# The tail of a two-image transformer tower: image 0's attention product ahead of image 1's on all engines

## The chip, the core and the metric

One NeuronCore of a Trainium2 chip. TensorE (PE) multiplies matrices into PSUM, eight banks of 512 fp32 columns; VectorE (DVE) and ScalarE (ACT) read PSUM and work element by element; GpSimd (POOL) does a few element-wise operations in SBUF; SyncE (SP) issues the transfers. The metric is the device time of one execution in microseconds, lower is better.

## What is computed

The first part is a two-layer vision transformer over two images (256 tokens each, width 128). The second part, the tail of the program, works on its output `h` of width 192: linear attention and a feed-forward network, each behind a normalisation and with a residual add.

```python
h = _L0_tok_ref(x, ...)                       # ends in: _ln(x, lnf_g, lnf_b) @ head_w + head_b
h = h + _L0_attn_ref(_layernorm(h), W_qkv, W_out, b_out)
h = h + _L0_ffn_ref(_layernorm(h), w_fc, w_proj, ...)

def _phi(x): return jax.nn.elu(x) + 1.0       # = max(min(exp(x), 1), x + 1)
# _L0_attn_ref, 12 heads of 16
q = _phi(q); k = _phi(k)
kv = jnp.einsum('bshd,bshm->bhdm', k, v)
z = 1.0 / (jnp.einsum('blhd,bhd->blh', q, k.sum(axis=1)) + EPS)
out = jnp.einsum('blhd,bhdm,blh->blhm', q, kv, z)
out = out @ W_out + b_out
# _L0_ffn_ref
h = new_gelu(jnp.einsum('bte,he->bth', x, W0) + b0)
out = jnp.einsum('bth,eh->bte', h, W1) + b1
```

## The kernel before

Everything is in one core; an image is two tiles (`t`) of 128 tokens. Each engine has its own list of instructions, written out by hand in order; an engine runs its list strictly in that order, and a line `engine.wait_ge(semaphore, n)` holds everything behind it on that engine. So the order of the lines is the schedule, and it is what the change edits. The two images (`i` = 0, 1) go through the same steps, interleaved.

The steps of the tail for one image, with the helper's name and the line that the profile gives:

- `turn` (L334), `gain` (ACT L1561), `head` (L446), `head_rows` (DVE L1041): the last normalisation of the first part and its head product; `h` is their result.
- `moments3`, `mean_and_variance`, `centre` (L939, L942, L959), `turn3` (L339, L340): moments, centring, transposition into a bank of 128 rows and a "rest" bank of 64 rows.
- `evict` of the rest (ACT L1558), `high_part3` (DVE L1046), `rest_low_part3` and `low_part3` (DVE L969): the transposed tile in two parts (high and low), so that the product keeps its precision. Semaphores `high3`, `low3`, later `high4`, `low4`.
- `qk3_high`, `qk3_low`, `v3_rows` (L454 to L459): query, key and value products of a tile. Banks `QK3_BANK`, `V3_BANK`.
- the features phi: `phi3_exp` (ACT L1593), `phi3_plus_one` (ACT L1597) and `phi3_max` (DVE L1056), each 128x384 for queries and keys of one tile. Their tiles lie in the memory named `embed_sb`.
- `turn_heads` of the queries (L483), `v3_to_sbuf` (ACT L1601), `context3` (L474), then `context3_masked` and `context3_sums` (DVE L1063, L1068).
- `numerators3` (L490), `denominator3`, `inverse3`, `attention3` (DVE L1077, L1081, L1084).
- `turn_heads` of the result (L483), its eviction (ACT L1558, tile `qkvw`), the output product `attend3` for each tile (L496, semaphore `out3_done`), `add_attention3` (DVE L1091).
- moments again, `inverse_deviation` on POOL (L1824), `normalise` (DVE L955), `turn3` (L339), high, rest and low parts once more.
- feed-forward: `fc3(i, c)`, six slices of five matmuls (L503 to L507), `gelu3` (ACT L1607) and `proj3(i, c, t)` (L510), then `add_ff3` (DVE L1095) and the stores.

In the order before, TensorE runs image 1's query, key and value products among image 0's attention, both tiles of image 0's output product before VectorE adds either, then image 1's features and context, and only then image 0's feed-forward slices, between which image 1's attention ends. VectorE makes image 1's high and low parts before image 0's denominator, and adds the attention of image 0 only when both tiles are done (`out3_done` 2).

## Time and profile before

| | us |
|---|---|
| median of three runs | 129.16 (128.75 to 129.81) |
| the profiled execution's own time | 129.22 |
| its span in the profile | 126.8 |
| PE busy | 117.3 (93%) |
| DVE busy | 77.0 (61%) |
| ACT busy | 62.9 (50%) |
| POOL busy | 45.9 (36%) |

The span reaches from the first instruction of the program to the last; the time of an execution has some 2.4 us around it. The granted clock of TensorE is 1.00 throughout, its higher level of 2.4 GHz. A row of the timeline gives the start in us from the span's beginning, the length, the engine, the line, what is written from what, the shape and how many instructions were merged; in square brackets stands the idle time of the engine ahead of it and who ended it. Matmuls overlap: the start of the next one, not the end of this one, tells how long TensorE was taken.

### The profile page before, as it was taken

What the parts mean: (1) busy time and instruction counts of PE and PEld (TensorE: products, weight loads), DVE (VectorE), ACT (ScalarE), POOL (GpSimd) and SP (SyncE); (2) the same over time, 40 slices, a digit from 0 to 9 for tenths busy, and PEclk for the clock granted to TensorE, in tenths of its full rate; (3) what the DMA queues carried; (4) which work ended last, traced back from release to release, by engine and by line L of the source; (5) the groups of instructions that cost most, each with busy time, mean ns of one, the idle gap of its engine ahead of it and who ended that gap; (6) DMA issues with size and microseconds to landing.
All of it is one profiled execution on the core that took longest, in us unless ns stands there. A gap on an engine that the chain in (4) does not pass through costs nothing.

```text
span 126.8 us, 2258 instructions
## 1 busy us (share of the span) xinstructions
PE 117.3 (93%) x852; PEld 101.2 (80%) x852; DVE 77.0 (61%) x244; ACT 62.9 (50%) x151; POOL 45.9 (36%) x56
## 2 busy tenths in 40 slices
PE   6999979999999999999999899977989988999991
PEld 6989968985978778997856689966777877998990
DVE  5000264996787766679999897639498377155002
ACT  4000142844579478194774876534871735423520
POOL 0000024034599833204939858475214032031000
PEclk9999999999999999999999999999999999999999
DMA  4999799999600000000000000000000000000101
GB/s 106 353 418 433 228 435 393 386 421 414 185 0 0 0 3 5 0 0 0 0 0 5 0 0 0 3 5 0 0 0 0 0 0 5 0 0 0 62 0 62
DMA packets 4171, 12.43 MB, mean 98 GB/s; under 512 B 473, under 2 KB 2105, under 8 KB 3906
## 3 DMA queue, kind: packets, MB, share of 16 engines
q1 hardware_dynamic: 4162, 12.31, 26.0%
q8 instruction: 6, 0.10, 0.3%
q14 instruction: 3, 0.02, 0.1%
HBM read 11.91 MB, written 0.39 MB: 97 GB/s over the span
## 4 chain that ended last, share of the span: by engine, by line
PE 65%; DVE 12%; DMA 9%; ACT 4%; issue 3%; SPq 3%; POOL 2%; DVEq 0%; ACTq 0%; POOLq 0%
DMA norm_rows_sb<-in_norm_rows 9%; PE bank L405 6%; PE bank L510 6%; PE bank L424 5%; PE bank L381 4%; PE bank L325 4%; PE bank L398 3%; PE bank L376 3%; SPq L265 3%; PE bank L346 3%; PE bank L412 2%; PE bank L358 2%; PE bank L496 2%; PE bank L334 2%; PE bank L390 2%
## 5 line engine op out<-in xcount | busy, mean ns | idle before, releaser
L1824 POOL TENSOR_TENSOR rstd<-mv,minus_half 128x2 f32<-128x2 f32 x14 | 10.0, 716 | 47.8 <-DVE mv L942 47.8
L1842 POOL TENSOR_TENSOR qn<-q,rqsum 128x512 f32<-128x512 f32 x8 | 8.3, 1042 | 10.5 <-DVE rqsum L1012 10.5
L1607 ACT ACTIVATE patches_sb<-bank,fcb 128x256 f32<-128x256 f32 x12 | 5.1, 469 | 10.5 <-PE bank L507 10.5
L1565 ACT ACTIVATE kexp<-bank,nkmax 128x256 f32<-128x256 f32 x16 | 7.5, 472 | 5.7 <-DVE nkmax L992 5.7
L405 PEld LDWEIGHTS bank<-cw,qT 128*128 128x128 f32 x64 | 8.0, 191 | 2.4 <-issue 1.5
L405 PE MATMUL bank<-cw,qT 128*128 128x128 f32 x64 | 8.9, 280 | 0.7 <-DVE x L1027 0.4
L510 PE MATMUL bank<-projw,patches_sb 128*128 128x192 f32 x48 | 9.4, 331 | 0.0
L325 PE MATMUL bank<-embed_sb 128*128 128x128 f32 x64 | 8.7, 291 | 0.3 <-DMA embed_sb<-in_embed 0.3
L424 PE MATMUL bank<-restw,hid 128*128 128x128 f32 x64 | 8.8, 281 | 0.1
L325 PEld LDWEIGHTS bank<-embed_sb 128*128 128x128 f32 x64 | 8.0, 200 | 1.1 <-DMA embed_sb<-in_embed 1.1
L1558 ACT ACTIVATE x<-bank 128x128 f32<-128x128 f32 x4 | 1.1, 282 | 14.4 <-DVE stats L936 14.4
L1581 ACT ACTIVATE hid<-bank,small_sb 128x256 f32<-128x256 f32 x16 | 6.5, 472 | 3.6 <-PE bank L419 3.6
L424 PEld LDWEIGHTS bank<-restw,hid 128*128 128x128 f32 x64 | 7.8, 191 | 0.6 <-issue 0.3
L936 DVE BATCH_NORM_STATS2 stats<-bank 128x6 f32<-128x128 f32 x4 | 1.1, 274 | 11.7 <-PE bank L330 11.6
L510 PEld LDWEIGHTS bank<-projw,patches_sb 128*128 128x128 f32 x48 | 7.6, 189 | 0.5 <-ACT patches_sb L1607 0.4
L381 PE MATMUL bank<-ktok,y 128*128 128x512 f32 x16 | 8.0, 612 | 0.0
L325 PE MATMUL bank<-embed_sb,patches_sb 128*128 128x128 f32 x64 | 7.9, 277 | 0.0
L325 PEld LDWEIGHTS bank<-embed_sb,patches_sb 128*128 128x128 f32 x64 | 7.5, 192 | 0.2 <-DMA patches_sb<-in_patches 0.2
L992 DVE TENSOR_REDUCE nkmax<-bank 128x2 f32<-128x512 f32 x8 | 5.4, 688 | 3.0 <-PE bank L365 2.9
L1834 POOL TENSOR_TENSOR xb<-x,rows_sb 128x256 f32<-128x256 f32 x8 | 5.8, 730 | 3.6 <-DVE xn L978 2.4
L969 DVE TENSOR_TENSOR yT_lo<-bank,yT_hi 128x256 fp32r<-128x256 f32 x12 | 5.1, 422 | 2.9 <-ACT yT_hi L1558 2.8
L1577 ACT ACTIVATE cw<-bank,rksum 128x128 f32<-128x128 f32 x16 | 4.8, 364 | 3.8 <-PE bank L398 3.8
(165 smaller groups left out, 333.0 us busy)
## 6 DMA issues: line engine op xcount, KB each, us to landing
embed_sb<-in_embed SPq DMA_DIRECT2D x3, 768.0 KB, 7.7
patches_sb<-in_patches SPq DMA_DIRECT2D x2, 1024.0 KB, 12.5
restw<-in_rest_w SPq DMA_DIRECT2D x2, 768.0 KB, 15.6
qkvw<-in_qkv_w SPq DMA_DIRECT2D x3, 256.0 KB, 11.7
qkvw<-in_qkv_w SPq DMA_DIRECT2D x1, 768.0 KB, 15.7
fcw<-in_fc_w SPq DMA_DIRECT2D x1, 768.0 KB, 18.3
embed_sb<-in_embed SPq DMA_DIRECT2D x1, 576.0 KB, 4.4
aqkvw<-in_aqkv_w SPq DMA_DIRECT2D x1, 576.0 KB, 12.2
```

The source lines that it names most:

```text
L325: mm = nc.tensor.matmul(CONV_BANK[i][t][:, 0:D], left, embed_sb[:, c, 0:D], start=(c == 0), stop=False)
L381: return nc.tensor.matmul(YK_BANK[s][:], y[s % IMAGES][:, t, :], ktok[:, t, :], start=(t == 0), stop=(t == TILES - 1))
L405: mm = nc.tensor.matmul(ATT_BANK[s][t][:, 0:D], qT[:, t, c * P:(c + 1) * P], cw[:, c, :], start=(c == 0), stop=(c == PAIRS - 1))
L424: mm = nc.tensor.matmul(FF2_BANK[s][t][:, 0:D], hid[:, c, t * P:(t + 1) * P], ff2w(s // IMAGES, c), start=(c == 0), stop=(c == FC - 1))
L510: return nc.tensor.matmul(PROJ3_BANK[i][t][:, 0:E], hid3[i][:, c, t * P:(t + 1) * P], projw[:, c, :], start=(c == 0), stop=(c == HC - 1))
L969: return nc.vector.tensor_tensor(lo, exact, hi.bitcast(F32), ALU.subtract)
L992: return nc.vector.tensor_reduce(nkmax[i][:, 2 * b:2 * b + 2], K_BANK[s][b][:].rearrange("p (c t) -> p c t", c=2), AX_X, ALU.max, negate=True)
L1565: return nc.scalar.activation(kexp[:, c, :], K_BANK[s][c // 2][:, (c % 2) * TOKENS:(c % 2 + 1) * TOKENS], ACT.Exp, bias=nkmax[i][:, c:c + ...
L1581: return nc.scalar.activation(hid[:, c, :], FF1_BANK[s][c // 2][:, (c % 2) * TOKENS:(c % 2 + 1) * TOKENS], ACT.Gelu, bias=col("ff1_b", s / ...
L1824: return nc.gpsimd.tensor_tensor(rstd[i][:], mv[i][:, :, 1], minus_half[:], ALU.pow)
L1834: return nc.gpsimd.tensor_tensor(xb[i][:], x[i][:], row.unsqueeze(1).to_broadcast([P, TILES, D]), ALU.add)
L1842: return nc.gpsimd.tensor_tensor(qn[:, t, :].rearrange("p (h d) -> p h d", h=HEADS), q[:, t, :].rearrange("p (h d) -> p h d", h=HEADS), rq ...
```

## The change

Only the tail is edited, from image 0's query and key products on.

- VectorE does two operations that ScalarE did: `phi3_plus_one(0, 0)` and `gain(1)`, with semaphores of their own (`phi3_plus_one_first`, `head_in_second`). ScalarE does one that VectorE did: the high part of image 0's second transposition (`evict(yT3_hi[0])`), so that `high4` comes from ScalarE for image 0 and `high4_second` from VectorE for image 1.
- TensorE runs image 0's value products before image 1's last transposition and head, image 0's numerators before `turn3(1)`, image 0's transposition of the attention and its output product before image 1's query and key products are complete, `turn3` of image 0's second normalisation before image 1's query transposition, and `fc3(0, 0)`, `fc3(0, 1)` before image 1's context. Image 1's context, numerators, transposition and output product stand between slices and projections of image 0.
- VectorE does image 0's context masks before image 1's moments, its denominator and attention before image 1's high and low parts, its add and second normalisation before image 1's features.
- `add_attention3(i, t)` waits for one tile (`out3_done` 1, 2, 3, 4) and so runs a tile at a time; the two tiles' products lie in different banks (`ATT3_BANK`).
- Banks of `TURN4`, `Q3` and `ATT3` move so that the new order has free banks.

```diff
@@ banks
-        TURN4_BANK = [bank[3], bank[5]]
+        TURN4_BANK = [bank[2], bank[5]]
-        Q3_BANK = [bank[6], bank[3]]
+        Q3_BANK = [bank[6], bank[1]]
-        ATT3_BANK = [bank[2], bank[7]]
+        ATT3_BANK = [(bank[2], bank[4]), (bank[7], bank[4])]
@@ TensorE
             qk3_low(0, 0).then_inc(qk3_done, 1)
+            qk3_low(0, 1).then_inc(qk3_done, 1)
+            v3_rows(0, 0).then_inc(v3_done, 1)
             pe.wait_ge(centred_last, 4)
             turn(TURNF_BANK[1], xn[1]).then_inc(last_turned, 1)
-            qk3_low(0, 1).then_inc(qk3_done, 1)
-            pe.wait_ge(head_in_ready, 2)
+            v3_rows(0, 1).then_inc(v3_done, 1)
+            pe.wait_ge(head_in_second, 1)
             head(1, 0).then_inc(head_done, 1)
...
+            pe.wait_ge(attention3_ready, 2)
+            turn_heads(AT3_BANK[0], att3[0]).then_inc(attention3_turned, 1)
             pe.wait_ge(high3, 2)
             qk3_high(1, 0)
-            pe.wait_ge(low3, 2)
-            qk3_low(1, 0).then_inc(qk3_done, 1)
             qk3_high(1, 1)
-            pe.wait_ge(attention3_ready, 2)
-            turn_heads(AT3_BANK[0], att3[0]).then_inc(attention3_turned, 1)
-            qk3_low(1, 1).then_inc(qk3_done, 1)
             pe.wait_ge(attention3_columns, 1)
             pe.wait_ge(loaded["aout"], 16)
             attend3(0, 0).then_inc(out3_done, 1)
             attend3(0, 1).then_inc(out3_done, 1)
...
             pe.wait_ge(low4, 1)
             fc3(0, 0).then_inc(fc3_done, 1)
             fc3(0, 1).then_inc(fc3_done, 1)
+            pe.wait_ge(v3_ready, 4)
+            context3(1).then_inc(context3_done, 1)
+            fc3(0, 2).then_inc(fc3_done, 1)
+            pe.wait_ge(q3_columns, 2)
+            pe.wait_ge(context3_ready, 4)
+            numerators3(1).then_inc(numerators3_done, 1)
+            fc3(0, 3).then_inc(fc3_done, 1)
+            pe.wait_ge(gelu3_ready, 1)
+            proj3(0, 0, 0).then_inc(proj3_done, 1)
+            pe.wait_ge(gelu3_ready, 2)
+            proj3(0, 0, 1).then_inc(proj3_done, 1)
             pe.wait_ge(attention3_ready, 4)
             turn_heads(AT3_BANK[1], att3[1]).then_inc(attention3_turned, 1)
-            fc3(0, 2).then_inc(fc3_done, 1)
-            pe.wait_ge(gelu3_ready, 1)
-            proj3(0, 0, 0).then_inc(proj3_done, 1)
+            proj3(0, 1, 0).then_inc(proj3_done, 1)
             pe.wait_ge(attention3_columns, 2)
             attend3(1, 0).then_inc(out3_done, 1)
             attend3(1, 1).then_inc(out3_done, 1)
...
@@ VectorE
+            def gain(i, bankof):
+                return nc.vector.tensor_scalar(yT[i], bankof[:, 0:TOKENS], col("lnf_g"), None, ALU.mult)
+            def phi3_plus_one(i, t):
+                return nc.vector.tensor_scalar(qk3p[i][:, t, :], QK3_BANK[i][t][:, 0:2 * E], rstd[i][:, t:t + 1], 1.0,
+                                               ALU.mult, ALU.add)
...
+            dve.wait_ge(phi3_exp_ready, 1)
+            phi3_plus_one(0, 0).then_inc(phi3_plus_one_first, 1)
+            dve.wait_ge(last_turned, 2)
+            gain(1, TURNF_BANK[1]).then_inc(head_in_second, 1)
...
-            dve.wait_ge(out3_done, 2)
+            dve.wait_ge(out3_done, 1)
             add_attention3(0, 0).then_inc(h_mid, 1)
-            add_attention3(0, 1).then_inc(h_mid, 1)
             dve.wait_ge(h_mid, 1)
             moments3(0, 0).then_inc(moments4_done, 1)
+            dve.wait_ge(out3_done, 2)
+            add_attention3(0, 1).then_inc(h_mid, 1)
...
@@ ScalarE
+            act.wait_ge(turned4, 1)
+            evict(yT3_rest[0][0:EB, :], TURN4_REST_BANK[0][0:EB, 0:TOKENS]).then_inc(rest_high4, 1)
+            evict(yT3_hi[0][:], TURN4_BANK[0][:, 0:TOKENS]).then_inc(high4, 1)
```

Three places of the order, before and of the change. Line numbers of the changed kernel are two or more higher for the same helper.

TensorE, where image 1's context product stands (L474 before, L476 now, from `v31`): before, it follows the transposition of image 1's queries (L483) and comes ahead of image 0's second transposition (L339, L340), image 1's numerators (L490) and image 0's first feed-forward slice (L503 on).

```order
L483 MATMUL bank3<-small_sb,embed_sb 96x128 x4
L474 MATMUL bank6<-v31,embed_sb 96x102 x4
L339 MATMUL bank3<-small_sb,xn0 128x128
L340 MATMUL bank4<-small_sb,xn0 64x128
L339 MATMUL bank3<-small_sb,xn0 128x128
L340 MATMUL bank4<-small_sb,xn0 64x128
L490 MATMUL bank6<-kv31,patches1_sb 128x102 x4
L503 MATMUL bank3<-yT3_hi0,fcw_hi 128x256
L504 MATMUL bank3<-yT3_hi0,fcw_lo 128x256
```

In the change:

```order
L485 MATMUL bank1<-small_sb,embed_sb 96x128 x4
L505 MATMUL bank3<-yT3_hi0,fcw_hi 128x256
L506 MATMUL bank3<-yT3_hi0,fcw_lo 128x256
L507 MATMUL bank3<-yT3_lo0,fcw_hi 128x256
L508 MATMUL bank3<-yT3_rest0,fcw_hi 128x256
L509 MATMUL bank3<-yT3_rest0,fcw_lo 128x256
L505 MATMUL bank3<-yT3_hi0,fcw_hi 128x256
L506 MATMUL bank3<-yT3_hi0,fcw_lo 128x256
L507 MATMUL bank3<-yT3_lo0,fcw_hi 128x256
L508 MATMUL bank3<-yT3_rest0,fcw_hi 128x256
L509 MATMUL bank3<-yT3_rest0,fcw_lo 128x256
L476 MATMUL bank6<-v31,embed_sb 96x102 x4
```

Image 0's first two feed-forward slices (ten matmuls, bank 3) now stand ahead of the context product of image 1.

VectorE, where image 0's denominator stands (`den30`, L1077 before, L1086 now): before, behind the high, rest and low parts of image 1 (`yT3_hi1`, `yT3_rest1`, `yT3_lo1`).

```order
L1063 TENSOR_TENSOR kv30<-bank1,small_sb 96x2x96
L1068 SCALAR_TENSOR_TENSOR kv30<-bank1,small_sb 96x2x6
L1046 CAST yT3_hi1<-bank0 128x256
L969 TENSOR_TENSOR yT3_rest1<-bank6,yT3_rest1 64x256
L969 TENSOR_TENSOR yT3_lo1<-bank0,yT3_hi1 128x256
L1077 TENSOR_SCALAR den30<-bank1 128x24
L1081 RECIPROCAL z30<-den30 128x24
L1084 TENSOR_TENSOR embed_sb<-bank1,z30 128x192 x2
```

In the change:

```order
L1072 TENSOR_TENSOR kv30<-bank1,small_sb 96x2x96
L1077 SCALAR_TENSOR_TENSOR kv30<-bank1,small_sb 96x2x6
L944 BN_AGGR mv1<-stats31 128x2
L941 BN_STATS stats31<-h1 128x6
L944 BN_AGGR mv1<-stats31 128x2
L961 TENSOR_SCALAR xn1<-h1,mv1 128x192 x2
L1086 TENSOR_SCALAR den30<-bank1 128x24
L1090 RECIPROCAL z30<-den30 128x24
L1093 TENSOR_TENSOR embed_sb<-bank1,z30 128x192 x2
```

Image 1's moments and centring (`stats31`, `mv1`, `xn1`) are now between the context sums and the denominator, and image 1's three parts have moved behind image 0's attention (L1093).

ScalarE, where the transposed attention of image 0 is evicted (tile `qkvw0`): before, between the features of image 1 (plus-one L1597, exponential L1593).

```order
L1597 ACTIVATE embed_sb<-bank3,ones,rstd1 128x384
L1593 ACTIVATE embed_sb<-bank3,rstd1 128x384
L1558 ACTIVATE qkvw0<-bank5 96x512
L1593 ACTIVATE embed_sb<-bank7,rstd1 128x384
L1597 ACTIVATE embed_sb<-bank7,ones,rstd1 128x384
```

In the change it comes ahead of all four of them:

```order
L1572 ACTIVATE qkvw0<-bank5 96x512
L1611 ACTIVATE embed_sb<-bank3,ones,rstd1 128x384
L1607 ACTIVATE embed_sb<-bank3,rstd1 128x384
L1607 ACTIVATE embed_sb<-bank7,rstd1 128x384
L1611 ACTIVATE embed_sb<-bank7,ones,rstd1 128x384
```

The features of image 1 (L1611, L1607) wait behind the eviction now.

## Rows read from the trace of the kernel before

**Rows 1.** Windows: stretch, its us, busy PE, PEld, DVE, ACT, POOL, granted clock, DMA.

```profile
104.00:112.00 8.00, 7.41 (x55) 6.80 (x54) 4.38 (x16) 3.71 (x7) 0.99 (x1) 1.00 0.01 2
112.00:120.00 8.00, 7.97 (x58) 7.58 (x59) 2.53 (x8) 2.99 (x8) 1.71 (x2) 1.00 0.08 25
```

**Rows 2.** Timeline: features of image 0's first tile, ScalarE and VectorE; columns as told above.

```profile
90.41 0.58 ACT L1593 ACTIVATE embed_sb<-bank,rstd 128x384 f32<-128x384 f32 x1 [0.52 <-PE bank L459]
...
90.89 0.47 ACT L1561 ACTIVATE y<-bank,small_sb 128x256 f32<-128x256 f32 x1
91.25 1.24 ACT L1597 ACTIVATE embed_sb<-bank,ones,rstd 128x384 f32<-128x384 f32 x2
...
91.95 0.56 DVE L1056 SCALAR_TENSOR_TENSOR embed_sb<-embed_sb 128x384 f32<-128x384 f32 x1 [1.80 <-ACT embed_sb L1597]
```

**Rows 3.** Timeline: image 0 from query transposition to its first feed-forward slice.

```profile
93.75 0.64 PE L483 MATMUL bank<-small_sb,embed_sb 128*96 128x128 f32 x4 [0.33 <-DVE embed_sb L1056]
93.94 0.19 DVE L942 BATCH_NORM_AGGREGATE mv<-stats 128x2 f32<-128x9 f32 x1
...
94.56 0.51 DVE L959 TENSOR_SCALAR xn<-h,mv 128x192 f32<-128x192 f32 x2
...
95.71 1.14 PE L490 MATMUL bank<-kv,patches_sb 96*128 96x102 f32 x8
...
97.06 0.17 DVE L1077 TENSOR_SCALAR den<-bank 128x24 f32<-128x24 f32 x1
...
98.28 0.64 PE L483 MATMUL bank<-small_sb,embed_sb 128*96 128x128 f32 x4
...
99.07 0.58 ACT L1558 ACTIVATE qkvw<-bank 96x512 f32<-96x512 f32 x1
...
99.71 1.57 PE L496 MATMUL bank<-aoutw,qkvw 96*128 96x192 f32 x8 [0.26 <-ACT qkvw L1558]
...
101.31 0.62 DVE L1091 TENSOR_TENSOR h<-bank,hb 128x192 f32<-128x192 f32 x2
...
101.85 0.61 DVE L939 BATCH_NORM_STATS2 stats<-h 128x6 f32<-128x192 f32 x2
...
102.38 0.31 DVE L942 BATCH_NORM_AGGREGATE mv<-stats 128x2 f32<-128x9 f32 x2
...
104.23 0.33 PE L339 MATMUL bank<-small_sb,xn 128*128 128x128 f32 x1
...
105.81 0.42 DVE L969 TENSOR_TENSOR yT_lo<-bank,yT_hi 128x256 fp32r<-128x256 f32 x1
...
106.29 0.39 PE L503 MATMUL bank<-yT_hi,fcw_hi 128*128 128x256 f32 x1 [0.49 <-DVE yT_lo L969]
```

**Rows 4.** Timeline: image 1 from its context product to its feed-forward and projections.

```profile
103.20 0.94 PE L474 MATMUL bank<-v,embed_sb 128*96 128x102 f32 x8 [0.39 <-ACT v L1601]
...
104.72 1.08 PE L490 MATMUL bank<-kv,patches_sb 96*128 96x102 f32 x8
...
108.90 1.49 PE L496 MATMUL bank<-aoutw,qkvw 96*128 96x192 f32 x8
...
111.87 0.20 DVE L942 BATCH_NORM_AGGREGATE mv<-stats 128x2 f32<-128x9 f32 x1
...
114.41 0.27 PE L339 MATMUL bank<-small_sb,xn 128*128 128x128 f32 x1
...
116.42 0.39 PE L503 MATMUL bank<-yT_hi,fcw_hi 128*128 128x256 f32 x1
...
118.81 2.11 PE L510 MATMUL bank<-projw,patches_sb 128*128 128x192 f32 x12
```

**Rows 5.** Timeline of ScalarE alone, around image 0's second transposition.

```profile
104.92 0.38 ACT L1558 ACTIVATE yT_rest<-bank 64x256 fp32r<-64x256 f32 x1 [1.30 <-PE bank L340]
105.32 1.28 ACT L1607 ACT_TABLE_LOAD   x1
```

93 lines of the change are left out of this document (41 added, 52 removed).

## The prediction

> **What bounds the kernel now.** I read the busy time by windows first. From 112 to 120 us TensorE is busy 7.97 us of 8 [rows 1]: there its own work sets the time, and only the start of that stretch can move. So I then read the timeline of the tail row by row, with what ended each wait, to see what sets that start. The last piece, image 1's six slices of the feed-forward product (L503 to L507) and its projections (L510), starts at 116.42 and runs to the end of the 126.8 us span without a wait that counts [rows 4]; nothing in it changes. So the forecast is one question: when does the first L503 of image 1 start in the changed kernel? The 10.38 us behind it are kept, and so are the 2.42 us that the profiled execution's own time (129.22 us) has over its span. That execution lies 0.06 us above the median of the runs, 129.16.
>
> Two chains lead there. Image 0's: features, transpose (L483), context, numerators (L490), denominator (L1077), attention, transpose, eviction, output product (L496), add (L1091), moments, normalisation, transpose (L339), high and low parts, first L503 at 106.29 [rows 3]. Image 1's goes the same way one lap later and ends at 116.42 [rows 4]. Before the change they are interleaved so that image 1's context product runs at 103.20, before image 0's feed-forward [rows 4].
>
> **Image 0's leg, walked with the new order.** Each hand-over is counted at the 0.03 to 0.06 us that the rows show between the end of one and the start of the next.
>
> Features: the first exponential ends at 90.99; then ScalarE does the gain and two plus-ones, and VectorE's first maximum waits 1.80 us for them, until 91.95 [rows 2]. Now VectorE does the first plus-one itself, from 91.02. No row has this form there; bounds are 0.56 (its own 128x384 maximum, from SBUF) and 0.62 (ScalarE's plus-one, 1.24 for two) [rows 2]; I take 0.58, nearer to the row of the same engine. The gain follows. Its bounds are 0.42 (VectorE's low part, 128x256 from PSUM [rows 3]) and 0.47 (ScalarE's own gain [rows 2]); I take 0.42. It also waits for image 1's transpose, which now stands behind the value product's first half on TensorE; I allow 0.15 for that (an estimate: eight matmuls stand ahead of it on TensorE), so a plus-one at its upper bound would cost nothing more. Two maxima, together 1.04: the transpose L483 starts at 93.27 instead of 93.75, 0.48 earlier.
>
> Perfetto Trace Analysis of the Trainium skill (Optimizing Scalar/DVE Operations) gives VectorE about 125 ns of overhead per instruction on PSUM and ScalarE about 51, which speaks against moving these two PSUM reads to VectorE. By it the moved gain would take 0.07 more than ScalarE's 0.47, 0.54 in all, and the leg would win 0.36 instead of 0.48, an estimate from that page. The rows here do not agree: VectorE's 256 columns from PSUM take 0.42 against ScalarE's 0.47.
>
> Numerators at 95.71 - 0.48 = 95.23, ending 1.14 later at 96.37 [rows 3]. Before, the denominator stood behind image 1's high, rest and low parts and started at 97.06. Now only image 1's moments and centring stand there, which took from 93.94 to 95.07 [rows 3], 1.13 us; started behind the context sums (95.2) they end just in time. So the denominator starts at 96.41, 0.65 earlier. To the transpose 1.22 (97.06 to 98.28), the transpose 0.64: eviction at 98.31 instead of 99.07, where it had stood behind an exponential of image 1. Output product at 98.95, 0.76 earlier.
>
> The add by tile: the product of both tiles takes 1.57; the first half of its eight matmul records is done after some 0.85. So the first add and its moments lie beside the second half. Behind the second tile's end (100.56) come one add 0.35, one moments 0.35, one mean 0.19 (the pairs' 0.62, 0.61 and 0.31 [rows 3], each of two that overlap by some 0.08) and two hand-overs: 101.53. Before, it was 102.69 [rows 3]. The lead is 1.16 us. Reciprocal deviation, normalisation and transpose are the same: L339 at 103.07. From there to L503 took 2.06 us [rows 3]. ScalarE now evicts the high part behind the rest, 0.38 each [rows 5], done 0.76 after the transpose; VectorE needs it for the low part only 0.89 after (104.92 to 105.81 [rows 3, 5]), so this costs nothing; were it 0.3 slower, 0.2. Image 0's first L503: 106.29 - 1.16 = 105.13.
>
> **Image 1's leg pays.** On TensorE its context product now stands behind the wait for image 0's low part and two feed-forward slices. Four slices take 2.39 us (116.42 to 118.81), so two take 1.20 [rows 4]: context at 106.33 instead of 103.20, 3.13 later. To its numerators 1.52, these 1.08: denominator at 108.97. 1.22 to the transpose, 0.64 for it, eviction 0.58, hand-overs 0.10: output product at 111.51 instead of 108.90. Here TensorE waits twice, about 0.2 before the transpose and 0.5 before the product, since the slices and projections put between them are shorter than the chain through VectorE and ScalarE.
>
> Then the add by tile gives part back: product 1.49, add, moments and mean as above, 114.01 instead of 112.07, that is 1.94 late. With 1.54 more, as from 102.69 to 104.23 [rows 3], the transpose could go at 115.55. TensorE is free a little later: from the product to that transpose it had 5.51 us of work (108.90 to 114.41), of which one slice (0.60) and two projections (twelve records in 2.11, two to a projection: 0.35 each) are done before now; 111.51 + 4.2 = 115.7. Before, the transpose ran at 114.41, 0.8 after its input was there, so the chain had slack; now it has none. Transpose 1.14 to 1.29 late; last L503 block at 117.56 to 117.71. I take the middle, **1.2 us later**.
>
> The other edits cost nothing: the table load of 1.28 [rows 5] now stands behind image 1's query eviction, some 0.3 us later than before, and its cover is that the first projection waits behind two more slices and two products of image 1; without that cover it would cost at most these 0.3. The moved banks only let the order be. GpSimd's and SP's queues keep their order.
>
> **The rivals.**
> 1. *Forecast: image 1's chain sets the end.* 129.22 + 1.2, rounded to the tenth above since hand-overs that no row has can only be longer than the shortest ones: 130.5; by the bounds (gain, plus-one, 0.03 or 0.06 at some fourteen hand-overs, the two ends above) 130.0 to 130.9.
> 2. *TensorE's work alone sets it, no change to be told.* If image 1's two waits (0.2 + 0.5) vanish because VectorE and ScalarE have nothing else there, TensorE still has the 10.13 us of 106.29 to 116.42 [rows 3, 4], plus image 1's context and numerators, about 0.8 + 0.9 (their 0.94 and 1.08 [rows 4] without the last records' drain, which the next matmul overlaps), which came before image 0's first slice and now come behind it. That is 105.13 + 11.8 = 116.9, or 0.5 late, and some 0.2 less for waits inside the 10.13: 129.5. For it speaks that TensorE is full from 112 [rows 1]; against it, that denominator to product takes 2.5 us by the rows and only some 1.9 us of work stands there.
> 3. *Faster.* Image 0's lead is larger, because VectorE's features and the overlapped add take less than I count. It decides at image 0's first L503: that must start before 104.6 (lead 1.7 or more) for the TensorE sum of rival 2 to end before 116.42, and at 103.3 the run is 1% faster, 127.9. Against it: the longest terms of the leg (0.64, 0.58, 1.57, 2.06) are unchanged instructions.
> 4. *The lead is not had, or the chain is longer.* If image 0's lead shrinks to 0.5 (the maxima wait for TensorE's turn, or the denominator for image 1's centring), every later time moves by 0.7: 131.1. The centring has only 0.1 us to spare there.
>
> **How the numbers follow.** Rival 1 0.58, rival 2 0.18, rival 3 0.08, rival 4 0.16. A difference of about 1% (1.3 us) is what a measurement of this kernel can tell from none; that line lies at 130.45 here, in the middle of the forecast's own range. So slower is 0.58 x 0.6 + 0.15 = 0.50; same is 0.58 x 0.4 + 0.18 + 0.01 = 0.42; faster 0.08. The range takes in rival 2 below and rival 4 above: 129.4 to 131.4, leaving out about 1 in 10 on each side.
>
> **What would show it.** In the profile after: image 0's L503 (there L505) near 105.1; image 1's context product behind two slices, near 106.3; TensorE waiting for VectorE's attention and for ScalarE's eviction of image 1, 0.7 together; image 1's transpose without slack behind the normalisation; image 1's first slice near 117.6, and the same 10.4 us behind it. I am wrong if that slice starts before 116.9, if image 0's lead is not about 1.2, or if VectorE's plus-one takes over 0.8. The granted clock should stay at 1.00 as in rows 1.

## The result, and the profile after

| | before | after |
|---|---|---|
| median of the runs | 128.98 us (128.67 to 129.81) | 130.24 us (130.01 to 131.99) |
| ratio to before | | 1.010 (95% interval 1.0075 to 1.0125) |
| span of the profiled execution | 126.8 us | 128.0 us |
| image 0's first feed-forward slice | 106.29 [rows 3] | 104.97 |
| image 1's first feed-forward slice | 116.42 [rows 4] | 117.59 |

The changed kernel is 1.0% slower. Image 0 is 1.32 us earlier, image 1 is 1.17 us later, and image 1 is the last. In two of the 11 executions of the changed kernel the mean granted clock was 0.987 instead of 1.00, and these took 131.22 and 131.99 us, the upper end of its row.

In the profile after, the line numbers are a few higher: L341 is the transpose, L485 the turn of heads, L476 the context, L492 the numerators, L498 the output product, L505 the first matmul of a feed-forward slice, L512 a projection, L1572 ScalarE's evictions. The two stretches of [rows 1], windows with busy PE, PEld, DVE, ACT, POOL, then granted clock and DMA:

```profile
104.00:112.00 8.00, 7.20 (x54) 6.19 (x55) 2.38 (x8) 4.75 (x11) 0.69 (x1) 1.00 0.01 2
112.00:120.00 8.00, 7.95 (x59) 7.51 (x59) 4.04 (x13) 2.06 (x6) 1.70 (x2) 1.00 0.08 25
```

From 112 us TensorE is as full as before, and the clock stays at its upper level: what was lost was lost ahead of that. The timeline of the features and of image 0 (start, us, engine, line, operation, what ended the wait ahead of it), which answers to [rows 2, 3]:

```profile
90.42 1.09 ACT L1607 ACTIVATE embed_sb<-bank,rstd 128x384 f32<-128x384 f32 x2 [0.52 <-PE bank L461]
...
91.11 0.62 DVE L1060 TENSOR_SCALAR embed_sb<-bank,rstd 128x384 f32<-128x384 f32 x1 [0.95 <-ACT embed_sb L1607]
...
91.42 0.66 ACT L1611 ACTIVATE embed_sb<-bank,ones,rstd 128x384 f32<-128x384 f32 x1
...
91.69 0.48 DVE L1057 TENSOR_SCALAR y<-bank,small_sb 128x256 f32<-128x256 f32 x1
...
92.10 1.02 DVE L1065 SCALAR_TENSOR_TENSOR embed_sb<-embed_sb 128x384 f32<-128x384 f32 x2
...
93.17 0.64 PE L485 MATMUL bank<-small_sb,embed_sb 128*96 128x128 f32 x4
...
95.12 1.11 PE L492 MATMUL bank<-kv,patches_sb 96*128 96x102 f32 x8 [0.61 <-DVE kv L1077]
...
96.27 0.18 DVE L1086 TENSOR_SCALAR den<-bank 128x24 f32<-128x24 f32 x1 [0.30 <-PE bank L492]
...
97.50 0.64 PE L485 MATMUL bank<-small_sb,embed_sb 128*96 128x128 f32 x4 [0.82 <-DVE embed_sb L1093]
...
98.18 0.59 ACT L1572 ACTIVATE qkvw<-bank 96x512 f32<-96x512 f32 x1 [1.09 <-PE bank L485]
...
98.82 1.57 PE L498 MATMUL bank<-aoutw,qkvw 96*128 96x192 f32 x8
...
101.22 0.20 DVE L944 BATCH_NORM_AGGREGATE mv<-stats 128x2 f32<-128x9 f32 x1
...
102.95 0.33 PE L341 MATMUL bank<-small_sb,xn 128*128 128x128 f32 x1 [0.43 <-DVE xn L957]
...
104.97 0.39 PE L505 MATMUL bank<-yT_hi,fcw_hi 128*128 128x256 f32 x1 [0.43 <-DVE yT_lo L971]
```

Image 0's chain now runs link by link, and TensorE waits at each: 0.61 ahead of the numerators and 0.82 ahead of the turn of the attention, where in the kernel before image 1's work stood. Image 1, which answers to [rows 4]:

```profile
106.22 0.86 PE L476 MATMUL bank<-v,embed_sb 128*96 128x102 f32 x8
...
108.84 0.18 DVE L1086 TENSOR_SCALAR den<-bank 128x24 f32<-128x24 f32 x1 [1.29 <-PE bank L492]
...
110.07 0.64 PE L485 MATMUL bank<-small_sb,embed_sb 128*96 128x128 f32 x4
...
111.39 1.57 PE L498 MATMUL bank<-aoutw,qkvw 96*128 96x192 f32 x8 [0.35 <-ACT qkvw L1572]
...
113.79 0.20 DVE L944 BATCH_NORM_AGGREGATE mv<-stats 128x2 f32<-128x9 f32 x1
...
114.80 0.67 DVE L957 TENSOR_SCALAR xn<-h,mv,rstd 128x192 f32<-128x192 f32 x2 [0.81 <-POOL rstd L1836]
...
115.58 0.28 PE L341 MATMUL bank<-small_sb,xn 128*128 128x128 f32 x1
...
117.59 0.39 PE L505 MATMUL bank<-yT_hi,fcw_hi 128*128 128x256 f32 x1
```

The context is 3.02 us later than before, the output product 2.49, the transpose 1.17. The normalisation ends at 115.47 and the transpose follows at 115.58. In the kernel before, the normalisation ended at 113.55, and the transpose at 114.41 followed only 0.86 us later; that slack is gone.

```profile
112.88 0.67 DVE L955 TENSOR_SCALAR xn<-h,mv,rstd 128x192 f32<-128x192 f32 x2 [0.82 <-POOL rstd L1824]
```

### The profile page after: what moved, and what is told of

Its sections match the earlier page's. It is cut to its first block, busy times and chain, and to the rows that moved or that the text cites. A ratio compares the mean times of both kernels' runs of the same rounds, so it can differ in the third digit from the quotient of the medians.

```text
span 128.0 us, 2259 instructions
## 1 busy us (share of the span) xinstructions
PE 117.1 (92%) x852; PEld 101.3 (79%) x852; DVE 77.7 (61%) x245; ACT 62.2 (49%) x150; POOL 46.6 (36%) x56
## 4 chain that ended last, share of the span: by engine, by line
PE 63%; DVE 12%; DMA 12%; SPq 5%; issue 3%; ACT 2%; POOL 1%; ACTq 0%
DMA patches_sb<-in_patches 12%; PE bank L407 6%; PE bank L426 5%; SPq L267 5%; PE bank L512 5%; PE bank L383 4%; PE bank L400 3%; PE bank L327 3%; PE bank L378 3%; PE bank L414 2%; PE bank L336 2%; PE bank L498 2%; PE bank L348 2%; PE bank L492 2%; PE bank L392 2%
## 5 line engine op out<-in xcount | busy, mean ns | idle before, releaser
L512 PE MATMUL bank<-projw,patches_sb 128*128 128x192 f32 x48 | 9.2, 329 | 0.0
L1572 ACT ACTIVATE x<-bank 128x128 f32<-128x128 f32 x4 | 1.1, 282 | 14.4 <-DVE stats L938 14.4
L512 PEld LDWEIGHTS bank<-projw,patches_sb 128*128 128x128 f32 x48 | 7.7, 189 | 0.3 <-ACT patches_sb L1621 0.2
```

The lines of the kernel that those rows point to most:

```text
L512: return nc.tensor.matmul(PROJ3_BANK[i][t][:, 0:E], hid3[i][:, c, t * P:(t + 1) * P], projw[:, c, :], start=(c == 0), stop=(c == HC - 1))
```

## The experiments

Two executions can differ by some tenths of a us ahead of the part that is changed. So beside the ratio of the runs to those of the kernel before, a table gives the **tail** of each profiled execution: from image 0's first transpose (87.53 in the changed kernel) to the end of the last add of the program (125.11 + 0.68 there). It is worked out from those two rows of each trace, so it stands for one execution. From the first transpose to image 1's output product the changed kernel, less_after and tile_back_1 run the same code, and their traces give 23.86, 23.89 and 23.92 us; differences of under 0.1 us say nothing.

| kernel | median us, ratio to before (95%) | tail us | against before |
|---|---|---|---|
| before | | 37.09 | |
| after | 130.24, 1.010 (1.0075 to 1.0125) | 38.26 | +1.17 |
| less_after | 130.23, 1.0086 (1.0052 to 1.0119) | 38.33 | +1.24 |
| less_before | 128.66, 0.9947 (0.9926 to 0.9969) | 36.57 | -0.52 |
| ctx_early | 129.43, 1.000 (0.9972 to 1.0027) | 37.09 | 0.00 |
| tile_back_1 | 130.86, 1.0135 (1.0101 to 1.0169) | 38.87 | +1.78 |
| filled | 130.50, 1.0111 (1.0079 to 1.0143) | 38.35 | +1.26 |
| feat_act | 132.28, 1.0201 (1.0155 to 1.0248) | 40.90 | +3.81 |
| tile_back | 131.96, 1.0153 (1.0111 to 1.0195) | 40.87 | +3.78 |
| high_dve | 130.90, 1.0109 (1.0063 to 1.0155) | 38.42 | +1.33 |
| tile_before | 129.17, 0.9991 (0.9967 to 1.0015) | 37.25 | +0.16 |
| feat_before | 129.51, 1.0021 (0.9990 to 1.0052) | 37.38 | +0.29 |
| pulled | 127.64, 0.9868 (0.9842 to 0.9895) | 35.68 | -1.41 |
| pulled_act | 129.27, 1.0016 (0.9980 to 1.0051) | 37.27 | +0.18 |

The theory of the prediction (A) is that image 1's attention chain sets the end. Its rival (B) is that TensorE's own work does, because image 1's context and numerators now stand behind image 0's first slices.

**Take work from TensorE.** Four projection matmuls left out between image 1's output product and its transpose, in both kernels.

```diff
-            proj3(0, 1, 1).then_inc(proj3_done, 1)
...
-            proj3(0, 2, 0).then_inc(proj3_done, 1)
-            proj3(0, 2, 1).then_inc(proj3_done, 1)
...
-            proj3(0, 3, 0).then_inc(proj3_done, 1)
```

> The changed kernel without four matmuls of image 0's second projection (hidden chunks 1 to 3: tile 1 of chunk 1, both tiles of chunk 2, tile 0 of chunk 3), which TensorE does between image 1's output product and image 1's transpose turn3(TURN4[1]); what they would add to image 0's output is left out. Each takes 0.32 to 0.33 us there, so TensorE has 1.3 us less to do ahead of that transpose. Theory A (image 1's attention chain sets the end): the two normalise instructions end at 115.47 us in the changed kernel and the transpose starts at 115.58; with less work in front it still starts at 115.5 to 115.6, TensorE waits about 1.3 us there, and the span stays 127.9 to 128.0 us (ratio to the kernel before 1.01). Theory B (TensorE's own work sets the end, since context and numerators of image 1 now stand behind the first fc3): the transpose starts at about 114.3 and the span is 126.7 (ratio 1.00).

> The kernel before without the same four matmuls of image 0's second projection (what they would add to image 0's output is left out): 1.3 us less for TensorE between image 1's output product and the transpose turn3(TURN4[1]). In the kernel before the two normalise instructions end near 113.6 us and the transpose starts at 114.41, so the chain has 0.75 us to spare there and TensorE's work is what comes last. Theory A: the transpose moves to where the chain allows it, about 113.65 to 113.7, and 0.7 of the 1.3 us comes back: span about 126.1 (ratio 0.994). Theory B: all 1.3 us come back, span 125.5 (ratio 0.99).

The rows with a wait, of less_after (the normalisation and the transpose) and then of less_before (a slice of image 0):

```profile
114.46 0.67 DVE L953 TENSOR_SCALAR xn<-h,mv,rstd 128x192 f32<-128x192 f32 x2 [0.82 <-POOL rstd L1832]
...
115.18 0.33 PE L341 MATMUL bank<-small_sb,xn 128*128 128x128 f32 x1 [1.05 <-DVE xn L953]
```

```profile
112.44 0.36 PE L503 MATMUL bank<-yT_hi,fcw_hi 128*128 128x256 f32 x1 [0.70 <-ACT patches_sb L1603]
```

In the changed kernel 1.3 us less work bought nothing: TensorE stood still for 1.05 us of it, waiting for image 1's normalisation. That is theory A: less work for TensorE does not help. But it was nearly a tie. Here the transpose starts 0.05 us behind the end of the normalisation (115.13), in the changed kernel 0.11 behind it, and without a wait of TensorE. So from the output product to the transpose (4.19 us) TensorE's work and the chain end within some 0.06 us of each other; the chain's lead is ahead of that, in the 0.35 us that TensorE waits for the product. In the kernel before the same cut bought 0.52 us, less than the 0.7 expected: behind the cut TensorE waited 0.70 us for ScalarE's GELU of image 0, a wait that I had not counted. So this run does not measure the slack of image 1's chain in the kernel before; it shows only that TensorE's work counts there.

**Bring image 1's chain forward.** In the changed kernel, context ahead of the first slice, ScalarE's values ahead of its evictions, numerators one slice earlier.

```diff
+            pe.wait_ge(v3_ready, 4)
+            context3(1).then_inc(context3_done, 1)
             pe.wait_ge(low4, 1)
...
-            pe.wait_ge(v3_ready, 4)
-            context3(1).then_inc(context3_done, 1)
-            fc3(0, 2).then_inc(fc3_done, 1)
...
+            fc3(0, 2).then_inc(fc3_done, 1)
```

> The changed kernel with image 1's context matmuls ahead of image 0's first fc3 (directly behind the turn of image 1's query features), the two evictions of image 1's values on ScalarE ahead of the evictions of image 0's second transpose, and image 1's numerators behind the second fc3 instead of the third. Image 0's lead up to there is kept. ScalarE is free at 103.12, so the values are there by 103.85, the context can run at 104.4 instead of 106.22, its masks at about 105.3, the numerators at 106.4 to 106.6 instead of 107.69. Theory A: the rest of image 1's chain moves with them as far as TensorE has room: its attention is turned about 0.9 us earlier, the output product at about 110.5 instead of 111.39, the last transpose at about 114.7 instead of 115.58, and the span is 127.0 to 127.3: most of the loss is undone (ratio to the kernel before 1.002 to 1.004). Theory B: only the 0.43 us for which TensorE waits ahead of the first fc3 is filled, and 0.2 of it is lost again because fc3's operands come later: span 127.6 to 128.0 (ratio 1.007 to 1.01).

TensorE's timeline of this kernel:

```profile
104.26 0.86 PE L476 MATMUL bank<-v,embed_sb 128*96 128x102 f32 x8
104.90 0.36 PE L505 MATMUL bank<-yT_hi,fcw_hi 128*128 128x256 f32 x1
...
106.16 1.03 PE L492 MATMUL bank<-kv,patches_sb 96*128 96x102 f32 x8
...
110.14 1.57 PE L498 MATMUL bank<-aoutw,qkvw 96*128 96x192 f32 x8 [0.35 <-ACT qkvw L1572]
...
114.32 0.28 PE L341 MATMUL bank<-small_sb,xn 128*128 128x128 f32 x1
```

The context starts 1.96 us earlier than in the changed kernel, the output product 1.25, the transpose 1.26, and the whole loss is gone: the tail is that of the kernel before. Theory A, and by more than I expected: I had thought TensorE short of room, but it still waits 0.35 ahead of the product. It also shows what image 0's lead is worth: its first slice starts at 104.90 here, 1.39 earlier than before (1.29 when counted from the first transpose), and the end is where it was.

**Lengthen image 1's chain.** In the changed kernel, image 1's attention added only when both tiles are there.

```diff
-            dve.wait_ge(out3_done, 3)
+            dve.wait_ge(out3_done, 4)
             add_attention3(1, 0).then_inc(h_mid, 1)
+            add_attention3(1, 1).then_inc(h_mid, 1)
```

> The changed kernel with image 1's attention alone added when both tiles' output products are done; image 0's adds stay by tile. Image 0's lead and everything up to image 1's output product stay as in the changed kernel. From the start of that product to the last transpose TensorE is never idle in the changed kernel (111.39 to 115.58, 4.19 us), and without four projections it waited 1.05 us there, so chain and work end within 0.25 us of each other. Theory A (image 1's chain sets the end): the chain behind the product is longer by the 0.4 to 0.67 us between the two adds, the last transpose starts 4.5 to 4.85 us behind the product's start, and the span is 128.3 to 128.7. Theory B (TensorE's own work alone): 4.19 us as before, span 128.0.

TensorE, image 1's product and transpose:

```profile
110.95 1.57 PE L498 MATMUL bank<-aoutw,qkvw 96*128 96x192 f32 x8 [0.35 <-ACT qkvw L1571]
...
115.67 0.33 PE L341 MATMUL bank<-small_sb,xn 128*128 128x128 f32 x1 [0.35 <-DVE xn L957]
```

From product to transpose 4.72 us against 4.19, and the tail is 0.61 longer: a longer chain behind the product moves the end, as A has it. Since chain and work were a tie there, this shows that the chain has no slack, not that the work has any.

**Put work into the waits of image 0's chain.** Three idle matmuls.

```diff
             context3(0).then_inc(context3_done, 1)
+            warm_up(bank[5], 1)
...
+            warm_up(bank[5], 2)
             pe.wait_ge(attention3_ready, 2)
```

> The changed kernel with three more matmuls on ones into a bank that is free there, whose result nobody reads: one in the 0.61 us for which TensorE waits ahead of image 0's numerators, two in the 0.82 us ahead of the turn of image 0's attention; each takes TensorE 0.32 to 0.33 us at full clock, 0.97 together. Theory A (TensorE's waits in image 0's chain are the chain's, and work put into them is free): numerators, turn and all behind them start when they did, span 127.9 to 128.1. Rival (TensorE's total work counts): span 128.9 to 129.0. Beside it, for the granted clock: in the changed kernel without image 0's features on VectorE TensorE waited 1.27, 0.61 and 0.82 us between 93 and 98.6 and its clock was 0.50 from 100 to 102; if such waits are what the clock falls after, the fuller stretch shows 1.00 throughout.

TensorE's timeline of this kernel, the added matmuls (L318) and the two links that waited:

```profile
94.15 0.51 PE L318 MATMUL bank<-ones 128*128 128x192 f32 x2
94.93 1.11 PE L492 MATMUL bank<-kv,patches_sb 96*128 96x102 f32 x8 [0.27 <-DVE kv L1079]
96.33 0.82 PE L318 MATMUL bank<-ones 128*128 128x192 f32 x4
97.31 0.64 PE L485 MATMUL bank<-small_sb,embed_sb 128*96 128x128 f32 x4 [0.17 <-DVE embed_sb L1095]
```

The matmuls (two records each) take up most of both waits, and the tail is longer by only 0.09 us. Work is free there. This is the room that image 1's work filled in the kernel before.

**What each edit is worth in the changed order.** First the features back on ScalarE, then both images' adds together, then image 0's high part on VectorE.

```diff
             phi3_exp(0, 0).then_inc(phi3_exp_ready, 1)
+            act.wait_ge(last_turned, 2)
+            gain(1, TURNF_BANK[1]).then_inc(head_in_ready, 1)
+            phi3_plus_one(0, 0).then_inc(phi3_plus_one_ready, 1)
```

> The changed kernel with the two moved feature instructions (one of image 0's plus-one tiles, and image 1's gain) back on ScalarE in their old order, all else as changed. In the kernel before the turn of image 0's query features starts at 93.75, in the changed one at 93.17. Theory A (image 1's chain hangs on the first fc3, which hangs on image 0's chain): the whole row of links is later by the 0.58 us or a little more, since image 0's features now stand directly in front of everything else: first fc3 at 105.5 or later, span 128.6 or more (ratio 1.014 or more). Theory B (TensorE's work behind the first fc3 sets the end and image 0's lead is slack): nothing changes by more than 0.2 us, span 127.9 to 128.2.

```diff
-            dve.wait_ge(out3_done, 1)
+            dve.wait_ge(out3_done, 2)
             add_attention3(0, 0).then_inc(h_mid, 1)
+            add_attention3(0, 1).then_inc(h_mid, 1)
```

> The changed kernel with both images' attention added only when the output products of both tiles are done, as in the kernel before; all else as changed. In the changed kernel the first add of image 0 starts at 99.78, the second at 100.45, and the last mean at 101.42 ends 0.97 us behind the second add's start; in the kernel before that stretch, both adds in one, took 1.38 us ([rows 3]: 101.31 to 102.69). So each image's chain is longer by 0.4 us, or by up to 0.67 if the first add's whole head start is lost. Theory A (image 1's chain sets the end and hangs on image 0's): both count, span 128.8 to 129.3 (0.8 to 1.3 us more than the changed kernel's 128.0). Theory B (TensorE's own work sets the end): image 0's lead and image 1's chain have slack, span 127.9 to 128.3.

```diff
+            dve.wait_ge(turned4, 1)
+            high_part3(0, TURN4_BANK[0]).then_inc(high4, 1)
...
-            evict(yT3_hi[0][:], TURN4_BANK[0][:, 0:TOKENS]).then_inc(high4, 1)
```

> The changed kernel with the high part of image 0's second transposed tile on VectorE again (0.42 us there, 0.36 on ScalarE), all else as changed. VectorE waits 0.22 us for ScalarE's eviction of the rest in front of its two low parts (104.06 and 104.49), ready since 103.85. With the high part in front, VectorE would do it from 103.85 (behind its second maximum) to 104.2, and the low parts at 104.25 and 104.7: the first fc3 is 0.1 to 0.25 us later. Theory A (the prediction's: the moved eviction is worth at most what VectorE waits, and image 1's chain follows the first fc3): span 128.0 to 128.25. Rival: the edit matters by its full 0.42 us, since low parts, fc3 and all of image 1 follow: span 128.4.

In the profiled executions of feat_act and of tile_back TensorE's granted clock fell, so their tails hold more than the edits. Windows of feat_act, then of tile_back:

```profile
98.00:100.00 2.00, 1.44 (x7) 1.43 (x8) 1.68 (x5) 0.64 (x2) 0.33 (x1) 0.70 0.00 0
100.00:102.00 2.00, 2.00 (x8) 2.00 (x7) 0.00 (x0) 0.10 (x1) 0.00 (x0) 0.50 0.00 0
```

```profile
104.00:106.00 2.00, 1.31 (x8) 1.05 (x9) 1.04 (x3) 1.97 (x6) 1.06 (x1) 0.94 0.00 0
106.00:108.00 2.00, 2.00 (x13) 2.00 (x12) 0.00 (x0) 1.51 (x3) 0.00 (x0) 0.50 0.00 0
```

Ahead of the fall both can be read. In feat_act the turn of image 0's query features starts 6.88 us behind the first transpose instead of 5.64: 1.24 later, more than the 0.58 expected, because in TensorE's new order ScalarE waits for image 1's turn ahead of its gain:

```profile
91.50 0.47 ACT L1570 ACTIVATE y<-bank,small_sb 128x256 f32<-128x256 f32 x1 [0.69 <-PE bank L336]
```

In tile_back image 0's transpose starts 4.73 us behind its output product (98.59 to 103.32) instead of 4.13, 0.60 later. There is no trace of these two kernels without the fall, but each has four executions at a granted clock of 1.00, with spans of 128.8 to 130.0 us (feat_act, median 129.6) and 128.6 to 129.9 (tile_back, 129.0); the medians of the kernel before beside them are 127.1 and 127.0. That is 2.5 and 2.0 us over the kernel before, where the changed kernel has 1.2: undoing the features costs some 1.3 us and undoing the adds some 0.8, with a spread of half a us. Both agree with A (128.6 or more; 128.8 to 129.3), and B's 128.3 at most is out. The high part on VectorE costs 0.16 us by the tail, within A's 0 to 0.25, too little for the ratio to tell.

**One edit alone in the order before.**

```diff
-        ATT3_BANK = [bank[2], bank[7]]
+        ATT3_BANK = [(bank[2], bank[4]), (bank[7], bank[4])]
...
-            dve.wait_ge(out3_done, 2)
+            dve.wait_ge(out3_done, 1)
```

> The kernel before with one part of the change alone: the attention added by tile (two banks for each image's output product), all orders else as before. Theory A (a link is worth something only where its chain is last): in the kernel before VectorE is at image 1's maximum until 101.3 when image 0's products come, so nothing starts earlier there, and in image 1 the last transpose waits for TensorE's own work, with 0.75 us to spare; gain between 0 and 0.1 us, or a loss of up to 0.2 by the new waits between VectorE's own instructions: span 126.7 to 127.0. Rival (the edit shortens each image's chain by 0.4 us or more wherever it stands): span 126.0 to 126.4.

```diff
+            phi3_plus_one(0, 0).then_inc(phi3_plus_one_first, 1)
+            dve.wait_ge(last_turned, 2)
+            gain(1, TURNF_BANK[1]).then_inc(head_in_second, 1)
...
-            gain(1, TURNF_BANK[1]).then_inc(head_in_ready, 1)
-            phi3_plus_one(0, 0).then_inc(phi3_plus_one_ready, 1)
```

> The kernel before with one part of the change alone: image 0's features as in the changed kernel (one plus-one tile and image 1's gain on VectorE, both maxima ahead of image 1's head rows, TensorE's order in this stretch as changed), all from the turn of image 0's query features on as before. That turn then starts about 0.58 us earlier, as in the changed kernel (93.17 against 93.75). Theory A (a link gains only where its chain is last): image 1's head rows, means and centre come behind both maxima on VectorE, as in the changed kernel, where the transpose of image 1 that needs them started 96.07 against 95.17; in the old order that transpose stands ahead of image 0's numerators, so TensorE waits there for 0.5 to 1 us and the lead is gone by the numerators: span 126.7 to 127.2, no gain. Rival (the 0.58 us go through to the end): span 126.2.

TensorE in feat_before:

```profile
93.36 0.64 PE L485 MATMUL bank<-small_sb,embed_sb 128*96 128x128 f32 x4
93.84 0.86 PE L476 MATMUL bank<-v,embed_sb 128*96 128x102 f32 x8
95.62 0.33 PE L341 MATMUL bank<-small_sb,xn 128*128 128x128 f32 x1 [0.92 <-DVE xn L961]
```

Neither gains: the ratios take in 1, the tails are 0.16 and 0.29 longer. In feat_before the turn does start 0.59 earlier (5.64 against 6.23 us behind the first transpose), and behind the context product TensorE then waits 0.92 us for image 1's centre.

**The opposite order.** Image 1 as close behind image 0 as its operands allow, image 0's remaining slices and projections behind that. Kept from the change: image 0's plus-one tile and the gain on VectorE, the adds by tile, the high eviction of image 0 on ScalarE, the banks. New here: one plus-one tile of image 1 on VectorE too, and the projections of both images interleaved at the end. TensorE's order against the kernel before, around the two images' attention:

```diff
             context3(1).then_inc(context3_done, 1)
-            pe.wait_ge(normalised4, 2)
-            pe.wait_ge(q3_columns, 2)
-            turn3(TURN4_BANK[0], TURN4_REST_BANK[0], xn[0]).then_inc(turned4, 1)
...
             numerators3(1).then_inc(numerators3_done, 1)
+            pe.wait_ge(normalised4, 2)
+            turn3(TURN4_BANK[0], TURN4_REST_BANK[0], xn[0]).then_inc(turned4, 1)
             pe.wait_ge(attention3_ready, 4)
             turn_heads(AT3_BANK[1], att3[1]).then_inc(attention3_turned, 1)
+            pe.wait_ge(low4, 2)
+            fc3(0, 1).then_inc(fc3_done, 1)
+            fc3(0, 0).then_inc(fc3_done, 1)
...
             attend3(1, 0).then_inc(out3_done, 1)
```

> The opposite order, with the same helpers and banks as the changed kernel: image 1's features, context, masks, numerators, attention and output product are pulled up as close behind image 0's as its operands allow (context of image 1 directly behind the turn of its query features, its numerators ahead of image 0's second transpose, its attention's turn ahead of image 0's first fc3, its output product behind two fc3 instead of four units of work), image 0's remaining fc3 and projections fill TensorE behind that, and the two images' projections are interleaved at the end. Some parts are kept from the change (one plus-one tile and the gain on VectorE, the high eviction of image 0 on ScalarE, the adds by tile). Theory A (the end is set by the later of image 1's chain and TensorE's work; with image 1 early, TensorE's work alone is left): in the kernel before TensorE waits about 0.6 us for image 1's values ahead of its context, 0.6 ahead of the first fc3 and 0.8 in front of image 0's turns and numerators; some 1 to 1.7 us of these close up, and the last transpose of image 1, ready 2 to 3 us earlier, is never waited for: span 125.1 to 126.0 (ratio 0.985 to 0.993). Theory B (only the work that stands behind the first fc3 counts, and image 0's early start is what shortens the program): image 0's output product and first fc3 come no earlier than in the kernel before, so nothing is gained: span 126.6 or more.

TensorE's timeline of this kernel:

```profile
101.41 0.86 PE L476 MATMUL bank<-v,embed_sb 128*96 128x102 f32 x8
102.79 1.14 PE L492 MATMUL bank<-kv,patches_sb 96*128 96x102 f32 x8 [0.52 <-DVE kv L1073]
...
105.20 0.64 PE L485 MATMUL bank<-small_sb,embed_sb 128*96 128x128 f32 x4 [0.80 <-DVE embed_sb L1089]
105.98 0.38 PE L505 MATMUL bank<-yT_hi,fcw_hi 128*128 128x256 f32 x1
...
111.49 0.27 PE L341 MATMUL bank<-small_sb,xn 128*128 128x128 f32 x1
```

This kernel beats both, by 1.3% against the one before. Image 1's context starts at 101.41 (before 103.20, after 106.22) and its last transpose at 111.49 (before 114.41, after 115.58), while image 0's first slice, at 105.98, is a full microsecond later than in the changed kernel. Behind 105.20 no row of TensorE shows a wait up to the last add. The span, 125.2, is what A expected (125.1 to 126.0), and not B's 126.6; and image 1's transpose is not waited for, as A said.

But A's sum was another: 1 to 1.7 us of TensorE's waits were to close up. Windows over the tail, of the kernel before, the changed kernel and pulled:

```profile
87.52:124.61 37.09, 34.34 (x234) 30.13 (x234) 18.93 (x64) 17.29 (x35) 7.00 (x9) 1.00 0.02 6
87.53:125.79 38.26, 34.30 (x234) 30.21 (x234) 19.62 (x65) 16.63 (x34) 7.71 (x9) 1.00 0.02 6
87.54:123.22 35.68, 32.94 (x234) 30.29 (x234) 20.21 (x66) 16.28 (x33) 7.00 (x9) 1.00 0.02 7
```

The changed kernel's loss is all in TensorE's idle time (38.26 - 34.30 = 3.96 against 2.75 us), but pulled's idle time is 2.74, as before. Its gain is in busy time, 1.40 us less for the same 234 records of matmuls. A busy row can hide a short stall, since the ends of matmuls are modelled: in the kernel before, 0.36 us pass from the projection at 116.06 to the next matmul, instead of the usual 0.16, and the rows show no wait of that length. The 48 records of projections, which pulled also puts in another order, are 0.6 of the 1.40, counted from start to start. So that image 1's early chain alone makes the gain is not shown; the interleaved projections were not run by themselves.

Then the same kernel with the three moved feature instructions (one plus-one tile of each image, and the gain) back on ScalarE:

```diff
             phi3_exp(0, 0).then_inc(phi3_exp_ready, 1)
+            act.wait_ge(last_turned, 2)
+            gain(1, TURNF_BANK[1]).then_inc(head_in_ready, 1)
+            phi3_plus_one(0, 0).then_inc(phi3_plus_one_ready, 1)
...
+            phi3_plus_one(1, 0).then_inc(phi3_plus_one_ready, 1)
```

> The kernel with image 1 pulled up (pulled), with the plus-one tiles of both images' features and image 1's gain back on ScalarE, where the kernel before has them; pulled itself has one plus-one tile of each image and the gain on VectorE. All orders else as in pulled. In pulled the turn of image 0's query features starts 5.49 us behind image 0's first transpose (93.03 against 87.54), in the kernel before 6.23 us (93.75 against 87.52). Theory A (chains decide, and image 1's now follows image 0's without a gap): the 0.7 us come back in image 0's features and up to 0.6 more in image 1's (one plus-one instruction of 0.66 us in a row on ScalarE), span 125.9 to 126.6. Rival (the order alone made the gain, the moved instructions nothing): span 125.1 to 125.4.

TensorE's two rows with the new waits:

```profile
94.38 0.64 PE L485 MATMUL bank<-small_sb,embed_sb 128*96 128x128 f32 x4 [0.69 <-DVE embed_sb L1061]
...
101.89 1.57 PE L498 MATMUL bank<-aoutw,qkvw 96*128 96x192 f32 x8 [0.74 <-ACT qkvw L1562]
```

The whole gain is gone (+1.59 in the tail, more than A's 0.7 to 1.3): the turn waits 0.69 us for the features, and the output product 0.74 for ScalarE's eviction, which is queued behind image 1's plus-one tiles. All of it is waits: TensorE's busy time in the tail is 32.92 us, that of pulled. So pulled's order with ScalarE's features gains nothing, two moved features in the order before (feat_before) gain nothing, and pulled's order with three moved features gains 1.3%.

## Why the prediction was right

The forecast was 130.5 us, slower by 1.2 us through image 1's chain. It came to 130.24, and the profiled execution's span grew by 1.2.

- **Features.** The plus-one took 0.62 on VectorE, my upper bound (0.58 taken), the gain 0.48 (0.42 taken, 0.47 the upper bound): both were set too low, by the row of the same engine, where ScalarE's rows for the same work, 0.66 and 0.47, lay nearer (0.66 is the single tile's row above). The 0.15 allowed for image 1's turn was not needed: it runs at 91.27 and the gain at 91.69. The turn starts at 93.17 instead of the 93.27 forecast; the errors cancel, which is luck. By the overheads of Perfetto Trace Analysis of the Trainium skill (Optimizing Scalar/DVE Operations), about 125 ns for VectorE and 51 for ScalarE on PSUM, I had estimated 0.54 for the gain; that is too high, and the trace's 0.48 lies between it and my 0.42.
- **Image 0's leg.** From there all links come 0.11 to 0.16 us ahead of the forecast: numerators 95.12 (95.23), denominator 96.27 (96.41), output product 98.82 (98.95), last mean's end 101.42 (101.53), transpose 102.95 (103.07), first slice 104.97 (105.13). The lead is 1.32 instead of 1.16.
- **Image 1's leg.** Context 106.22 (106.33), denominator 108.84 (108.97), output product 111.39 (111.51), last mean's end 113.99 (114.01), transpose 115.58 (115.55 to 115.7), slice 117.59 (117.56 to 117.71). The waits of TensorE were mis-sized: 0.2 and 0.5 were named, and the trace shows none ahead of the turn at 110.07 and 0.35 ahead of the product. The last step was right by luck in part: of two bounds for the transpose, the chain's 115.55 and TensorE's 115.7, the later one holds, yet I took the middle. The 4.2 us of work behind the product were right (4.19 measured); the product itself came 0.12 earlier than summed, and that made up for it.
- **The other edits.** ScalarE's high eviction costs nothing, and by the tail of high_dve it gains 0.16; I had counted no gain. The table load is hidden, as said, and no row of TensorE waits for a GELU there. It starts 0.08 us later than before (105.32 [rows 5]), not 0.3:

```profile
105.40 1.28 ACT L1621 ACT_TABLE_LOAD   x1
```

- **From span to time.** The profiled execution took 130.23 us, 2.2 above its span; I had kept the 2.42 of the execution before, and rounded up. These 0.2 to 0.3 us are the difference between 130.5 and the result.
- **Rivals.** Rival 2, TensorE's work alone, falls with less_after and with the 0.35 us that TensorE waits ahead of image 1's product. Yet it stood close: behind that product, chain and work are a tie. From image 0's first slice to image 1's (104.97 to 117.59) TensorE took 12.27 us without the 0.35, where rival 2 had summed 11.8; in ctx_early the same work took 11.7 (104.26 to 116.33, less 0.35). So about half a us of the changed kernel's busy time there goes with its order, and is no fixed work. Rival 3 was excluded by the lead, 1.32 and not 1.7, and ctx_early says more: even with the lead and without image 1's loss nothing is gained. Rival 4 did not come: VectorE is done with the centring 0.30 us before the denominator's input is there, where I had counted 0.1.

The prediction did not ask about the opposite order. Keeping image 0's lead and bringing image 1's context forward (ctx_early) only gives the loss back; the best kernel, pulled, has image 1 early and keeps 0.3 us of image 0's lead.

## What to carry to other kernels

Where two chains share the engines, find the one that ends last, and do not pay for the other's lead with it: 1.3 us of lead for image 0 was worth nothing, and 3 us of delay for image 1's context cost 1.2. An edit that shortens a link must be tried in the order in which that link is last: moved features and adds by tile gained nothing in the old order, cost some 1.3 and 0.8 us when undone in the new one, and the moved features made the difference of 1.3% with image 1 pulled up. A wait of the engine that is the bound is room for the other chain's work, and should be filled with the work that is late next. And compare the engine's busy time too: short stalls can stand in it, and pulled's gain was there and not in the waits that the rows show.

## What the hardware showed besides

**GpSimd beside VectorE.** The addition of the output bias on GpSimd took 1.72 us in the changed kernel, while VectorE ran the two maxima, whose two inputs are both in SBUF, from 102.82 to 103.84:

```profile
102.98 1.72 POOL L1850 TENSOR_TENSOR hb<-h,projb 128x384 f32<-128x384 f32 x1 [0.78 <-DVE xn L957]
```

In pulled, where no maximum runs beside it, it takes 1.00. The other traces agree: 1.71 or 1.72 in the eight kernels with this overlap, 0.99 to 1.00 in the six without it.

```profile
103.77 1.00 POOL L1845 TENSOR_TENSOR hb<-h,projb 128x384 f32<-128x384 f32 x1 [0.78 <-DVE xn L953]
```

SBUF — State Buffer of the Trainium skill (SBUF: two separate sides) says that GpSimd and a VectorE instruction with two SBUF inputs lock each other out for a whole instruction. The trace agrees on GpSimd's side: of the 0.86 us of overlap it lost 0.72. The maxima, the first of which had started before, kept their length (1.02 for the two, as for image 0's at 92.10, where GpSimd is idle). It did no harm here, since nothing waits for that sum until the last add.

**The clock.** In feat_act TensorE waited 1.27, 0.61 and 0.82 us between 93 and 98.6, and in the windows above its granted clock was then 0.70 and 0.50, the lower of its two levels (1.2 GHz); in tile_back it waited 1.03, 0.28 and 0.44 between 102.3 and 105.4, and then ran at 0.50 from 106 to 108. While the clock was down the output product took 2.28 us instead of 1.57. Over all executions, the mean granted clock was 0.986 or 0.987 in 14 of the 81 of kernels with the changed or the opposite order, and in none of the 104 with the order before (the kernel before, less_before, tile_before, feat_before). So the fall goes with the order; that the waits cause it is not shown, for pulled, with one such execution of six, has no more idle time in its tail than the kernel before. Filled, with the same chain and fuller stretches, shows 1.00 in all its six executions, and so do nine of eleven of the changed kernel: too few to tell whether filling prevents it.
